# Dividing a search for row maxima between a feed-forward stage and an attention stage, and moving a gate by 25 steps

## The reference, cut to what matters

```
xn  = layernorm(x)                          # x is 4 x 1024 x 256, float32
q, k, v = split(xn @ w_qkv)                 # 16 heads of 16
scores  = where(causal, (q / 4) @ k.T, -1e10)
s   = softmax(scores) @ v @ w_out
g   = silu(ffn(xn))                         # 6 blocks:  x = gelu(x @ W1.T + B1) @ W2.T + B2 + x,
                                            # a layernorm with gain and bias after the first five
out = x + s * g
```

## Time and profile before

| | us |
|---|---|
| median of 3 runs | 1562.08 |
| runs | 1559.25, 1562.08, 1563.09 |
| the profiled execution, its own time | 1559.22 |
| its span, first to last instruction | 1557.3 |
| busy PE, DVE, ACT, POOL | 1534.7, 1220.1, 958.3, 386.8 |
| mean granted clock | 0.998 |

### The profile page before, as it was taken

The page is one execution under the profiler, slowest core; times in us unless marked ns, Lnnn a source line. Parts: engine busy times, 40 slices in busy tenths (PEclk is TensorE's granted clock), DMA queues, the critical chain, the costliest instruction groups (busy, mean ns, idle before and its releaser), DMA issues. The chain is left out here.

```text
span 1557.3 us, 28828 instructions
## 1 busy us (share of the span) xinstructions
PE 1534.7 (99%) x11004; PEld 1201.6 (77%) x11004; DVE 1220.1 (78%) x2695; ACT 958.3 (62%) x1404; POOL 386.8 (25%) x323
## 2 busy tenths in 40 slices
PE   8999999999999999999999999999999999999998
PEld 7889888888888888887888888888888744444443
DVE  7845988889888888888898888887666577777753
ACT  4445555565655555645556555555455599898995
POOL 1102322222212222222222231221101133333334
PEclk9999999999999999999999999999999999999999
DMA  8979547557454114142141241230711255475432
GB/s 297 322 215 246 148 123 188 133 137 197 121 127 126 54 50 116 48 107 65 44 116 49 65 115 37 67 103 28 205 56 36 82 159 165 143 199 172 125 110 69
DMA packets 110434, 193.38 MB, mean 124 GB/s; under 512 B 13676, under 2 KB 81260, under 8 KB 102636
## 3 DMA queue, kind: packets, MB, share of 16 engines
q1 hardware_dynamic: 110296, 191.54, 43.2%
HBM read 136.70 MB, written 79.95 MB: 139 GB/s over the span
## 5 line engine op out<-in xcount | busy, mean ns | idle before, releaser
L776 ACT ACTIVATE m_hid<-m_h_ps,m_b1s 128x512 f32<-128x512 f32 x384 | 264.3, 688 | 489.9 <-PE m_h_ps L880 439.2
L852 DVE TENSOR_TENSOR m_hidl<-m_hid,m_hidh 128x512 fp32r<-128x512 f32 x384 | 351.7, 922 | 189.3 <-ACT m_hidh L779 180.0
L1130 ACT ACTIVATE a_prob<-a_st_ps 128x1024 f32<-128x1024 f32 x288 | 278.5, 1023 | 33.6 <-PE a_st_ps L1222 28.5
L893 PE MATMUL m_y_ps<-shared,m_hidh 128*128 128x256 f32 x1536 | 274.1, 281 | 1.9 <-DVE xres L811 1.9
L779 ACT ACTIVATE m_hidh<-m_h_ps,m_b1s 128x512 fp32r<-128x512 f32 x384 | 261.1, 680 | 0.0
L880 PE MATMUL m_h_ps<-xth,shared 128*128 128x512 f32 x768 | 254.5, 392 | 1.7 <-PEq L296 1.7
L893 PEld LDWEIGHTS m_y_ps<-shared,m_hidh 128*128 128x128 f32 x1536 | 235.5, 188 | 19.0 <-issue 9.5
L893 PE MATMUL m_y_ps<-w2h,m_hidh 128*128 128x256 f32 x768 | 218.6, 285 | 1.7 <-DVE xres L811 1.7
L893 PE MATMUL m_y_ps<-shared,m_hidl 128*128 128x256 f32 x768 | 213.0, 277 | 0.0
L893 PE MATMUL m_y_ps<-w2l,m_hidh 128*128 128x256 f32 x768 | 212.9, 277 | 0.0
L893 PE MATMUL m_y_ps<-w2h,m_hidl 128*128 128x256 f32 x768 | 212.8, 277 | 0.0
(11 more groups left out here) (127 smaller groups left out, 2545.3 us busy)
## 6 DMA issues: line engine op xcount, KB each, us to landing
turned_rows<-apart SPq DMA_DIRECT2D x47, 512.0 KB, 2.7
apart<-turned_rows SPq DMA_DIRECT2D x188, 128.0 KB, 3.1
mq<-q_stacks SPq DMA_DIRECT2D x16, 896.0 KB, 7.1
mk<-k_stacks SPq DMA_DIRECT2D x16, 896.0 KB, 10.4
shared<-k_stacks SPq DMA_DIRECT2D x14, 896.0 KB
shared<-q_stacks SPq DMA_DIRECT2D x14, 896.0 KB
q_stacks<-q_parts SPq DMA_DIRECT2D x96, 128.0 KB
k_stacks<-k_parts SPq DMA_DIRECT2D x96, 128.0 KB
```

The source lines that it names most:

```text
L776: nc.scalar.activation(hid[n % 2][:], h_ps[n % 2][:], ACT.Gelu, bias=b1s[i % 2][:, k:k + 1])
L852: nc.vector.tensor_tensor(hidl[n % 4][:], hid[n % 2][:], hidh[n % 4][:].bitcast(F32), ALU.subtract).then_inc(low_done, 1)
L893: m = nc.tensor.matmul(y_ps[:, j, :], h[n % 4][:, j * P:(j + 1) * P], w[par][:, k, :], start=(k == 0 and j % 2 == 0 and h is hidh and w is ...
L1130: nc.scalar.activation(to, scores, ACT.Exp).then_inc(exp_done, 1)
```

## The change

The attention gets exactly one visit in each of its first 124 steps, and the feed-forward stage all others. So 180 visits (90 pairs) are in `mlp` and 124 in `attend`: nine visits, of group 9, change stage. Pair j in `mlp` now goes to place 135 j / 90, so each slot from 3 to 47 has its visits at chunks 0 and 2, and none at chunk 6. The loads of group m + 2 and the stores that hang on a visit move with it; the load of group 11 goes from the end of `mlp` to step 12 of `attend`. `GATE_AT` becomes the first step with a tile, `min(TILES_AT)` = 43, so the tanh is behind the exponentials of step 43 and the product at the end of step 45, behind that step's mixing.

```diff
+NS = 9
+STEPS_SEARCHED = NS * (N_GROUPS - 2) - 2
...
-        VISITS = search.at[AHEAD, 0]
+        VISITS = len(search.visits) - STEPS_SEARCHED
...
-NS = len(STEPS)
+assert len(STEPS) == NS
...
-GATE_AT = 2 * NS
...
 END = max(TILES_AT) + 5
+GATE_AT = min(TILES_AT)
...
-    VISITS = range(search.at[AHEAD, 0], len(search.visits))
-    AT = {}
-    for v in VISITS:
-        AT.setdefault((NS * (N_GROUPS - 2) - 2) * (v - VISITS[0]) // len(VISITS), []).append(v)
+    VISITS = range(len(search.visits) - STEPS_SEARCHED, len(search.visits))
+    AT = {step: [v] for step, v in enumerate(VISITS)}
```

## The result

The changed kernel takes 1549.9 us (median of 5 runs, 1548.83 to 1552.93) where the kernel before, run beside it, takes 1562.05 (5 runs, 1559.25 to 1563.09). The ratio is 0.9939, with a 95% interval of 0.9927 to 0.9951: 9.5 us less, between 7.7 and 11.4. (The two medians themselves lie 12.2 us apart; single runs of one kernel spread over about 4 us.) I had forecast 6.5 us less. The profiled execution took 1549.9 us with a span of 1548.0, 9.3 us less than the span before, so it can be used to account for the difference.

What follows compares the result with a forecast made beforehand. PE was taken to bound the feed-forward stage and ACT's exponentials the attention steps. 4.06 + 1.5 + 0 + 1.2 - 0.3 = 6.5 us less than 1562.08 gave 1555.6 us, 8 in 10 between 1551 and 1561.5.

Steps and rivals of the forecast that it cites:

- Nine visits leave the feed-forward stage: Feed-forward stage: four full pairs at 0.86 us and a single visit at 0.63 us fewer, 4.06 us saved.
- The new places: Feed-forward slots with visits only at chunks 0 and 2: 1.5 us saved, range +3.6 to -4.5 us.
- the four stalls: Chunk 2 of slots 7, 16, 25, 34: 0.9 us each behind visits 0 and 1; two go, 1.8 us saved.
- The new kinds at chunk 2: Feed-forward chunk 2: visit pairs that never stood there cost 0.3 us in all, bounds nothing and 6.3 us.
- The moved loads: Feed-forward DMA queue: the 2.9 us lost at slot 25 is kept, slot 17 being alike; 0, between -2.9 and +2.9.
- The attention's visits: Attention: nine visits fill empty steps that were no shorter; cost 0.3 us for DVE, bounds 0 and 3.9 us.
- Rival A: Attention: single rests let DVE and PE recover, so each new visit costs 0.43 us; gain 2.9 us, 1559.2; chance 0.12.
- The gate: Attention: 1.70 us go at steps 18 to 24, 0.5 us come at the new place; 1.2 us saved, +0.4 to +1.7.
- The sum: Whole kernel: all terms together give 6.5 us less, from the median 1562.08 to 1555.6 us.
- B: Feed-forward: DVE becomes the bound in each slot's first half; 13 us lost, less the 6.5: 1568.6 us; chance 0.06.
- C: Feed-forward DMA queue: one or two more slots lose 2.9 us; gain 0.7 to 3.6 us, 1558.5 to 1561.4; chance 0.12.
- D: Attention: DVE's product costs at step 45 what it costs now; gain 5.3 less perhaps 0.5, 1557 us; chance 0.10.

Runs made afterwards that it cites:

- experiment 2: The changed kernel with its 180 feed-forward visits at the old places, three places in a slot; ratio to the kernel before 0.9975 (1556.09 us).
- experiment 3: The changed kernel with three pairs of visits moved from chunk 2 to chunk 6 in slots 16, 17 and 35; slot 17's second pair took 6.46 us.
- 4: The kernel before with the visits at chunk 6 of slots 6, 15, 24 and 33 moved to chunk 2; the stalled pairs took 5.63 to 5.73 us.
- experiment 5: The kernel before with the next slot's columns issued ahead of the search's loads on SP's queue; feed-forward stage 3.9 us shorter, at 1233.67 us.
- experiment 1: The kernel before with only the gate moved to step 43, visits unchanged; 1556.67 us in one profiled execution.

## Why the prediction was right, and where it was not

**Nine visits leave the feed-forward stage, 4.06 us: right.** With the old places the stage was 3.3 us shorter, with 1.0 us lost at its empty end (experiment 2), and full pairs still last 6.35 us and empty ones 5.49.

**The new places, 1.5 us: right in sign, too small.** The step that failed is the reading of the earlier trace rows: I put the four stalls down to the pair (0, 1) at chunk 0, since each followed one, and kept two of them. Slot 43 has the same pair and no stall, and I had not looked at it, nor at the visits at chunk 6 that each stalled slot also followed. Experiments 3 and 4 make and (but for 0.8 us) unmake the stall with those visits alone. All four went: 3.6 us and not 1.8. The new kinds at chunk 2, for which I had taken 0.3 us and up to 6.3, cost 0.35 us at each of slots 9 and 28, for (7, 8), and about 0.06 for (0, 1) and (1, 2). I had counted (7, 8) twice; it comes to chunk 2 three times, the third in slot 47. Set against what these kinds had cost at their old places, about 0.3 us remain, as taken.

**The moved loads, 0: wrong, and worth 3.0 us between these two profiles.** That is 0.1 us beyond the bound of 2.9 that I gave. I had counted right that slot 17 takes the part of slot 25, and ACT did wait there, 2.2 us. What I had not asked is what covers such a wait. With chunk 6 empty it costs PE nothing; with chunk 6 filled and a wait of 3.7 us it cost 0.7 (experiment 3), and in the four profiles with the old places and the old order, with waits of 4.3 to 5.1 us, 2.3 to 3.0. How much of the difference is the cover and how much the shorter wait stays open. What makes the wait itself is shown in experiment 5.

**The attention's visits, 0.3 us: too small.** The plain steps are as forecast, 35.85 us for steps 0 to 17. But without the gate the attention takes 307.92 us, and 306.95 with all the old rests and the gate hidden (experiment 1): 1.0 us for the nine visits and the new order of kinds, of which 0.4 is step 107. The sum of worst bounds in the prediction took 0.7 us here, where the term itself had 3.9; the measured 1.0 lies between. In steps 0 to 42, which had held three of the nine rests, the two differ by 0.04 us, as the empty steps had shown directly; DVE's queue further on was the part that I only guessed. Rival A, which would have had 3.9 us here, is out.

**The gate, 1.2 us: right in its mechanism, too large.** 1.64 off at the old place, 0.7 on at the new one and 0.25 at step 81, so it brought 0.7 us, within the range of 0.4 to 1.7. It is the full visit behind the product that costs, as argued, for the same move in front of a cheap visit costs nothing (experiment 1).

**The sum.** The forecast was low by 2.8 us of span because two terms of the feed-forward stage were short, by 1.8 and 3.0 us, and two of the attention were off the other way, by 0.7 and 0.5. About 1 us more was given back ahead of slot 1 and behind slot 46, where no term stood, and slots 2 and 3, which vary from profile to profile, happened to be 0.5 us shorter. That the number came out as near as it did is in part luck.

**Rivals.** B, DVE as the bound at chunks 0 and 2 of each slot, did not come: from slot 4 on no slot lasts more than 24.04 us. In slot 26, with (0, 1) at chunk 2, DVE is busy 21.44 of 23.75. C, more slots that lose to the columns, is the opposite of what happened. D, the gate only moved, is not what happened either, but the 0.7 us that the gate brought lie nearly as close to its nothing as to my 1.2.

## What to carry to other kernels

A stall has more than one neighbour: list what all its cases have in common, the slot before included, and look for a place with the same neighbour and no stall, before charging it to the dearest thing beside it. When work is spread over places of a loop, the place that is left empty can be worth as much as the count (here 3.6 us against 4.06), since it lets late data and a late engine catch up before the next fixed wait. On an in-order DMA queue, issue what the next iteration needs ahead of a large load that has an iteration or more to spare.

## What the runs showed of the hardware that I had not expected

A backlog on DVE was passed on by way of POOL: DVE itself had caught up, but POOL's addition of 2.40 us had started 0.7 us later, and DVE's next product of two SBUF operands lasted 2.81 us instead of 2.10, and 0.69 when alone. And four transfers of 128 KB that stood behind 1.8 MB of loads and the gains and biases kept ACT waiting for 2.2 to 5.1 us, and not at all behind either alone, while the DMAs moved 168 and 178 GB/s in the two windows looked at (before at slot 25, after at slot 17), where the kernel's first 60 us show 304.
